# Attention over edges: a fourth chunk of weights turned by DMA in heads 4 and 5, and other places for the next tile's loads

## The reference

```python
q = ((x @ Wq[l].T + bq[l]) * scaling).reshape(n, H, DH)
k = (x @ Wk[l].T).reshape(n, H, DH)
v = (x @ Wv[l].T).reshape(n, H, DH)
scores = jnp.einsum('ehd,ehd->eh', q[tgt], k[srcidx])
m = jax.ops.segment_max(scores, tgt, num_segments=n)
p = jnp.exp(scores - m[tgt])
s = jax.ops.segment_sum(p, tgt, num_segments=n)
w = p / (s[tgt] + 1e-16)
agg = jax.ops.segment_sum(w[:, :, None] * v[srcidx], tgt, num_segments=n)
attn = agg.reshape(n, D) @ Wo[l].T + bo[l]
```

## Time and profile before

| | us |
|---|---|
| median of 3 runs | 3416.27 |
| lowest, highest | 3409.2, 3417.36 |
| span of the profiled execution | 3423.3 |
| PE busy in the span | 3052.8 (89%) |
| DVE, POOL, ACT busy | 2274.0, 2149.5, 1953.9 |

### The profile page before, as it was taken

How to read it: one execution, slowest core, us unless ns; L and a number is a source line. 1 busy time by engine, 2 the same in 40 slices (tenths; PEclk the granted TensorE clock), 3 DMA queues, 4 the chain that set the end, 5 groups by cost and what they waited for, 6 DMA issues and landing times. The chain is left out here.

```text
span 3423.3 us, 72330 instructions
## 1 busy us (share of the span) xinstructions
PE 3052.8 (89%) x24802; PEld 2399.2 (70%) x24802; DVE 2274.0 (66%) x6951; ACT 1953.9 (57%) x3918; POOL 2149.5 (63%) x1979
## 2 busy tenths in 40 slices
PE   2368999978869999999999989989999999999985
PEld 2124665545547888888888877767888888888874
DVE  8594433432337888888887853227888888888856
ACT  0124444433337777777777721227777778777724
POOL 1686778777527777777777710007777777777734
PEclk9999999989989999999999999999999999999987
DMA  9666666545589999999999921239999999989851
GB/s 371 98 129 158 124 118 131 113 93 98 90 201 175 166 170 166 170 163 172 163 168 160 156 75 29 52 70 181 169 165 167 166 172 168 169 165 175 151 119 60
DMA packets 1297462, 496.76 MB, mean 145 GB/s; under 512 B 1237240, under 2 KB 1262865, under 8 KB 1291408
## 3 DMA queue, kind: packets, MB, share of 16 engines
q1 hardware_dynamic: 1156197, 460.22, 67.6%
q0 software_dynamic: 133120, 0.80, 4.1%
q10 hardware_dynamic: 7788, 31.21, 2.7%
HBM read 153.55 MB, written 80.48 MB: 68 GB/s over the span
## 5 line engine op out<-in xcount | busy, mean ns | idle before, releaser
L1476 DVE CUSTOM_DVE_ANT_0 prob<-s_ps,mask 125x500 f32<-125x500 f32 x1600 | 1058.9, 673 | 277.8 <-PE s_ps L1323 201.8
L1253 POOL TENSOR_TENSOR staged<-prob,staged 125x500 f16<-125x500 f32 x960 | 1061.7, 1112 | 166.3 <-ACT staged L1247 103.8
L1413 ACT ACTIVATE prob<-prob,neg_max 125x1000 f32<-125x1000 f32 (+1 forms) x960 | 954.6, 994 | 117.5 <-DVE scrap L1482 114.7
L1323 PE MATMUL s_ps<-keys,queries 128*125 128x500 f16 x3200 | 944.5, 377 | 40.3 <-DMA queries<-q_tiles 27.4
L529 POOL DMA_INDIRECT counts<-count,cell x320 | 654.5, 2045 | 257.9 <-issue 96.4
L1354 PEld LDWEIGHTS o_ps<-values,across 125*125 125x125 f16 x7680 | 590.3, 138 | 196.8 <-issue 51.7
L1354 PE MATMUL o_ps<-values,across 125*125 125x128 f16 x7680 | 606.5, 222 | 33.8 <-DMA across<-staged 33.0
L1247 POOL CAST staged<-prob 125x500 f16<-125x500 f32 x640 | 385.5, 602 | 368.2 <-ACT prob L1413 238.5
L1489 DVE TENSOR_TENSOR p_lo<-t_ps,p_hi 125x500 f16<-125x500 f32 x640 | 432.1, 675 | 91.5 <-ACT p_hi L1423 91.1
L1334 PE MATMUL t_ps<-identity,prob 125*125 125x125 f32 x2560 | 411.8, 283 | 2.7 <-ACT agg L1433 2.5
L1423 ACT CAST p_hi<-t_ps 125x500 f16<-125x500 f32 x640 | 361.0, 564 | 85.1 <-PE t_ps L1334 84.5
(11 more groups left out here) (159 smaller groups left out, 3676.2 us busy)
## 6 DMA issues: line engine op xcount, KB each, us to landing
mask<-bias_rows SPq DMA_DIRECT2D x200, 218.8 KB
counts<-xt ACTq DMA_DIRECT2D x8, 3054.0 KB, 37.3
keys<-counts SPq DMA_DIRECT2D x40, 546.9 KB
bias_rows<-edge_bias SPq DMA_DIRECT2D x20, 1093.8 KB
queries<-q_tiles SPq DMA_DIRECT2D x80, 250.0 KB, 3.9
pair_row<-pair_flat SPq DMA_DIRECT2D x40, 437.5 KB
across<-staged SPq DMA_TRANSPOSE x960, 3.3
q_tiles<-q_both SPq DMA_DIRECT2D x80, 125.0 KB, 3.0
```

Source lines behind the costliest of these rows:

```text
L1253: engine.tensor_tensor(here[0:P, BPC:2 * BPC, 0:P], prob[u % PROBS][:, k * KC:(k + 1) * KC].rearrange("p (s c) -> p s c", s=BPC), here[0:P ...
L1323: mm = pe.matmul(s_ps[n % SB][:, 0:KC], lhsT=queries[b][:, h, part, :], rhs=keys[:, h, c * KC:(c + 1) * KC], start=(part == 0), stop=(part ...
L1413: act.activation(here, here, ACT.Exp, bias=neg_max[u % 4][:, :], accum_out=sums[u // H % 2][:, u % H, piece:piece + 1]).then_inc(exped, 1)
L1476: dve.tensor_tensor_reduce(out=prob[u % PROBS][:, at], in0=s_ps[n % SB][:, 0:KC], in1=bias[b][:, at], scale=1.0, scalar=MASKED, op0=ALU.ad ...
```

## The change

In heads 4 and 5 of every tile (`MORE_AT`) chunk 1 is turned by DMA too, and PE turns only chunk 3. POOL makes both halves of chunk 1 in its stage. It signals on the semaphores of chunk 0 (`STAGED_BY`). Counts that were products are now looked up in lists. The rings keep their sizes: three stages, four `across`. The next tile's loads move: the first half of the queries and mask chunk 0 to head 7 of the tile before (for tile 1, to the start), the second half to head 0, mask chunks 1, 2, 3 to heads 1, 2, 3, and chunk 4 to head 5. Head 4 and head 6 load nothing.

```diff
-BY_DMA = (0, 2, 4)
-BY_PE = tuple(k for k in range(NKC) if k not in BY_DMA)
-HIGH_BY = {0: "POOL", 2: "POOL", 4: "ACT"}
-LOW_BY = {0: "POOL", 2: "POOL", 4: "POOL"}
+MORE_AT = (4, 5)
+HIGH_BY = {0: "POOL", 1: "POOL", 2: "POOL", 4: "ACT"}
+STAGED_BY = {0: 0, 1: 0, 2: 2, 4: 4}
...
+def by_dma(u):
+    return (0, 1, 2, 4) if u % H in MORE_AT else (0, 2, 4)
+
+
+def by_pe(u):
+    return tuple(k for k in range(NKC) if k not in by_dma(u))
...
-                        before, chunk = dma_chunk_at(n - ACROSS)
-                        sp.wait_ge(weighted, NKC * before + chunk + 1)
-                    sp.wait_ge(low_staged[k], U0 + u + 1)
+                        sp.wait_ge(weighted, weighted_by(DMA_CHUNKS, n - ACROSS))
+                    sp.wait_ge(low_staged[STAGED_BY[k]], staged_by(u, k))
...
+                def begin_next(t):
+                    if t < NT:
+                        if t > 1:
+                            sp.wait_ge(maxed, U0 + H * (t - 1))
+                        load_queries(t, 0)
+                        load_mask(t, 0)
+
+                def go_on(t, h):
+                    if t < NT:
+                        if h == 0:
+                            load_queries(t, 1)
+                        elif h <= 3:
+                            load_mask(t, h)
+                        elif h == 5:
+                            load_mask(t, 4)
...
                 for u in range(UNITS):
...
+                    t, h = u // H, u % H
+                    if h == H - 1:
+                        begin_next(t + 2)
+                    else:
+                        go_on(t + 1, h)
...
-                    for k in BY_DMA:
+                    for k in by_dma(u):
                         turn(u, k)
...
-                        for k in BY_DMA:
-                            reached(dve, low_staged[k], U0 + u - PROBS + 1)
+                        if u >= PROBS:
+                            for k in by_dma(u - PROBS):
+                                dve.wait_ge(low_staged[STAGED_BY[k]], staged_by(u - PROBS, k))
```

More of the change, by code:

```diff
@@ L87 @@
 ACROSS = 4
+def by_dma(u):
+    return (0, 1, 2, 4) if u % H in MORE_AT else (0, 2, 4)
+def by_pe(u):
+    return tuple(k for k in range(NKC) if k not in by_dma(u))
+DMA_CHUNKS = [(u, k) for u in range(UNITS) for k in by_dma(u)]
+PE_CHUNKS = [(u, k) for u in range(UNITS) for k in by_pe(u)]
+DMA_AT = {chunk: n for n, chunk in enumerate(DMA_CHUNKS)}
+PE_AT = {chunk: n for n, chunk in enumerate(PE_CHUNKS)}
+STAGED_AT = {}
+for signal in (0, 2, 4):
+    for n, chunk in enumerate(c for c in DMA_CHUNKS if STAGED_BY[c[1]] == signal):
+        STAGED_AT[chunk] = n
+STAGED_COUNT = {signal: sum(STAGED_BY[k] == signal for u, k in DMA_CHUNKS) for signal in (0, 2, 4)}
 EXTRA = {(1, 4): ("T", 0), (2, 2): ("T", 1), (3, 2): ("O", 0), (3, 4): ("O", 1), (4, 2): ("O", 2), (4, 4): ("O", 3)}
@@ L93 @@
     for k in range(NKC):
-        if k in BY_PE:
+        if k in by_pe(u):
             USERS.append(("P", u, k))
@@ L1189, in attention @@
         stages_cleared = sem("stages_cleared")
-        high_staged = {k: sem(f"high_staged{k}") for k in BY_DMA}
-        low_staged = {k: sem(f"low_staged{k}") for k in BY_DMA}
+        high_staged = {k: sem(f"high_staged{k}") for k in STAGED_COUNT}
+        low_staged = {k: sem(f"low_staged{k}") for k in STAGED_COUNT}
         crossed = [sem(f"crossed{r}") for r in range(ACROSS)]
@@ L1207, in pe_chunk, with staged_by, weighted_by @@
         def pe_chunk(u, k):
-            return len(BY_PE) * (U0 + u) + BY_PE.index(k)
+            return len(PE_CHUNKS) * layer + PE_AT[u, k]
         def dma_chunk(u, k):
-            return len(BY_DMA) * (U0 + u) + BY_DMA.index(k)
-        def dma_chunk_at(n):
-            return n // len(BY_DMA), BY_DMA[n % len(BY_DMA)]
+            return len(DMA_CHUNKS) * layer + DMA_AT[u, k]
+        def staged_by(u, k):
+            return STAGED_COUNT[STAGED_BY[k]] * layer + STAGED_AT[u, k] + 1
+        def weighted_by(chunks, n):
+            in_layer, n = divmod(n, len(chunks))
+            u, k = chunks[n]
+            return NKC * (UNITS * in_layer + u) + k + 1
         def user_done(engine, n):
@@ L1222, in user_done @@
             if what == "P":
-                engine.wait_ge(bank_read, len(BY_PE) * (UNITS * in_layer + where) + BY_PE.index(part) + 1)
+                engine.wait_ge(bank_read, len(PE_CHUNKS) * in_layer + PE_AT[where, part] + 1)
             elif what == "T":
@@ L1247, in high_to_stage @@
             copy(staged[n % STAGES][0:P, 0:BPC, 0:P],
-                 prob[u % PROBS][:, k * KC:(k + 1) * KC].rearrange("p (s c) -> p s c", s=BPC)).then_inc(high_staged[k], 1)
+                 prob[u % PROBS][:, k * KC:(k + 1) * KC].rearrange("p (s c) -> p s c", s=BPC)).then_inc(high_staged[STAGED_BY[k]], 1)
         def low_to_stage(engine, u, k):
             here = staged[dma_chunk(u, k) % STAGES]
-            engine.wait_ge(high_staged[k], U0 + u + 1)
+            engine.wait_ge(high_staged[STAGED_BY[k]], staged_by(u, k))
             engine.tensor_tensor(here[0:P, BPC:2 * BPC, 0:P],
                                  prob[u % PROBS][:, k * KC:(k + 1) * KC].rearrange("p (s c) -> p s c", s=BPC),
-                                 here[0:P, 0:BPC, 0:P], ALU.subtract).then_inc(low_staged[k], 1)
+                                 here[0:P, 0:BPC, 0:P], ALU.subtract).then_inc(low_staged[STAGED_BY[k]], 1)
         with nc.Block() as block:
@@ L1259, in _, with load_queries @@
             def _(sp):
[L1260 to L1263, removed]
+                def load_queries(t, half):
+                    sp.dma_start(queries[t % 2][64 * half:64 * half + 64, :, :, :].rearrange("d h s n -> d (h s n)"),
+                                 q_tiles[t * DH:(t + 1) * DH, :]).then_inc(q_loaded[t % 2], 16)
                 def load_mask(t, c):
@@ L1278, in turn @@
                                            ).then_inc(crossed[n % ACROSS], 16)
-                load_queries(0)
+                def begin_next(t):
[12 more added lines that the diff above has]
+                            load_mask(t, 4)
+                for half in range(2):
+                    load_queries(0, half)
                 for c in range(NKC):
                     load_mask(0, c)
+                begin_next(1)
                 for u in range(UNITS):
[L1284 to L1295, removed]
-                    for k in BY_DMA:
+                    t, h = u // H, u % H
[3 more added lines that the diff above has]
+                        go_on(t + 1, h)
+                    if t == 0 and h == NKC + 1:
+                        sp.dma_start(wo_sb[:, :, :].rearrange("p c d -> p (c d)"), g["wo"][layer * 128:(layer + 1) * 128, :]
+                                     ).then_inc(wo_loaded, 16)
+                    for k in by_dma(u):
                         turn(u, k)
@@ L1303, in _ @@
                 for u in range(UNITS):
-                    for k in BY_DMA:
+                    for k in by_dma(u):
                         if HIGH_BY[k] == "POOL":
                             high_to_stage(pool, pool.tensor_copy, u, k)
-                        if LOW_BY[k] == "POOL":
-                            low_to_stage(pool, u, k)
+                        low_to_stage(pool, u, k)
             @block.tensor
@@ L1420, in high_half @@
                     if m >= PB:
-                        unit, at = divmod(m - PB, len(BY_PE))
-                        act.wait_ge(weighted, NKC * unit + BY_PE[at] + 1)
+                        act.wait_ge(weighted, weighted_by(PE_CHUNKS, m - PB))
                     act.copy(p_hi[m % PB][:, :], t_ps[r][0:P, 0:KC]).then_inc(p_high, 1)
@@ L1468, in add_bias @@
                             dve.wait_ge(mask_loaded[b], BOTH * NKC * ((T0 + u // H) // 2 + 1))
-                        for k in BY_DMA:
-                            reached(dve, low_staged[k], U0 + u - PROBS + 1)
+                        if u >= PROBS:
+                            for k in by_dma(u - PROBS):
+                                dve.wait_ge(low_staged[STAGED_BY[k]], staged_by(u - PROBS, k))
+                        elif layer > 0:
+                            for signal in STAGED_COUNT:
+                                dve.wait_ge(low_staged[signal], STAGED_COUNT[signal] * layer)
                         apart(dve, g["waits_met"])
@@ L1522, in statistics @@
                                      xt[:, o, c * CH:(c + 1) * CH]).then_inc(bn_chunks, 1)
[L1524 to L1528, removed]
                 for u in range(2):
@@ L1533, in _ @@
                     maximum(u)
-                for step in range(NKC):
-                    stage_lows(0, step)
                 for u in range(UNITS):
@@ L1543, in _ @@
                             read_low(u - 1)
-                        stage_lows(u, k + NKC)
-                        if u + 1 < UNITS:
-                            stage_lows(u + 1, k)
                         step = extra_before(u, k)
```

## The result

The changed kernel takes 3568.6 us (median of four) where the kernel before, timed beside it, takes 3415.9: a ratio of 1.0452, with a 95% interval of 1.0436 to 1.0468, or 153 us more. Three of its four executions took 3564.6 to 3571.1 us; the fourth took 5299.5 at a granted clock of 0.556, where the others had 0.968, and the ratio leaves it out. Its profiled execution has a span of 3568.9 us. Forecast were 3500 and a range of 3400 to 3575: the sign and the mechanism held, the forecast size was 84 us of the 153.

What follows compares the result with a forecast made beforehand. PE looked like the bound, with the three-stage staging ring a second loop close behind. A tile going from 48.9 to 51.0 us, +2.1 over 40 tiles, adds 84 us: 3500 in the runs, range 3400 to 3575.

Steps and rivals of the forecast that it cites:

- The ring of three stages: Staging buffers filled, subtracted, issued, landed, refilled: a second loop beside PE, needing 45.0 us of a 48.9 us tile.
- The length of a turn: One stage's cycle: copy to end of subtraction 1.79, issue 0.20, landing 3.51, next copy 0.12; sum 5.62 us.
- the 3.9 us that I called spare: Per tile in the kernel before: tile of 48.9 us against 45.0 us for 8 turns on three stages.
- The turns: Staging: 26 chunks instead of 24 on three stages, 8.67 turns of 5.62 us, 48.7 us a tile if never idle.
- six tenths: Share of the spare 3.9 us taken to remain, 2.3 us, giving 51.0 us a tile; ends 48.7 and 52.6.
- The held copy: ACT's copy of chunk 4 in heads 4 and 5 waits for chunk 0's landing: 1 to 3 us, twice a tile.
- It holds: SP with two more issues of 1.44 us: from 40.9 to 43.8 us of a tile, still carried.
- rival D: The DMA engines fill, queues form and landings grow by perhaps 0.3 us, to over 3.7: 3604 us; chance 0.10.
- DMA share higher: Expected sign in the changed kernel: the DMA engines' share above the 0.93 of the stretch before.
- The moved loads: Same 12 issues in other heads: counted as nothing; PE's waits for transposes, at most 23 us in all, could be won.
- PE's 39 us: Chunk 1's PE transposes gone in heads 4 and 5: 80 x 0.49 us, all exposed while PE is the bound.
- Rival A: Landings hide, PE's 39 us come out: 3377 us; needs a turn under 5.52 us; chance 0.18.

## Why the prediction was right, and what it mis-sized

**The bound.** The ring of three stages as a second loop beside PE was right, and it was read from one landing and one copy 0.15 us behind it. It was more than that already: a fourth stage gave the kernel before 35 us, where PE's waits for transposes were to be worth 23 at most.

**The length of a turn.** 5.62 us lies beside the 5.55 of the run with two stages, but that is in part luck: landings were shorter there (3.35 us), and the time still holds 0.19 us of wait. In the kernel before a turn took 6.09 us on average. Of its distance from 5.62, 0.28 us is a stage standing free (0.40 less my 0.12 for the next copy), the rest is the issue (0.28, I had estimated 0.20), the fill (1.86, not 1.79) and the landing (3.55, not 3.51). So only 2.2 of the 3.9 us that I called spare were idle stages.

**The turns.** 26 / 3 turns of 5.62 are 48.7 us, and the tile took 52.5. The term that I mis-sized is the idle time that the ring keeps: I took 2.3 of 3.9 us, six tenths between two ends with no row for it, and 3.8 was left over my turns. That was my upper end (52.6), and is the difference between 84 and 144 us. By the table 1.7 of these 3.8 us are stages standing free in the changed kernel (8.67 x 0.20), and the other 2.1 are turns that take longer than I had summed, which no full ring would have filled. Why the 1.7 remain can only be argued: a delay in the ring may come back to it through the exponentials, which come in PE's rhythm, since PE waits for the ring.

**The held copy.** Right as a row, though larger than the 1 to 3 us that I saw: on average over the inner tiles ACT's wait grew from 0.7 to 3.1 us in head 4 and from 0.3 to 4.3 in head 5, the longest of all heads. Wrong as a cause. It was my reason for the larger share; with the copy moved to POOL the time stays (3579).

**POOL, SP, DMA.** "It holds" was right for the load, as the run with transposes beside four stages shows. It was wrong to count nothing: with three stages two more issues are delays in the ring, 67 us by themselves. In the changed kernel they may overlap with what the two more stage uses cost: its issue part grew by 0.06 us a turn only, some 20 us in all. Landings did not grow (3.55 us on average before and after, and D wanted over 3.7), so rival D is out. The sign "DMA share higher" did not come, since the tile grew with the transposes.

**The moved loads.** I took nothing. Alone they cost 26 us, through the ring: 0.08 us more a turn, 8 turns, 40 tiles. Beside the fourth chunk no such cost is seen. The sum for the whole change was hardly touched.

**PE's 39 us.** The size is about right where the rings are wide: from the kernel before with four stages to the changed one with four stages and five `across`, PE's busy time falls by 0.83 us a tile (47.57 to 46.74), of my 0.98. Its idle time rises by 0.24 (0.27 to 0.51). That the 39 us would be "all exposed as long as PE is the bound" was too much: 17 came out. In the changed kernel itself PE's busy time doesn't fall (3069.6 us after 3052.8), and why it doesn't stays open.

**The rule weighed.** The Trainium skill, page DMA: Bandwidth & Descriptors, section Rules for kernel authors, says to issue a DMA early and wait on its semaphore late, so that its fixed cost overlaps. Here the buffer waits as well, and the runs side with the row: the same chunks take 3569 us with three stages and 3391 with four.

**Rival A** wanted landings under 3.41 us and a ring with room. It had neither: they took 3.55.

## What to carry to other kernels

Before work is moved to a path of copy, transfer and use, count its buffers: turn time over number of buffers is the path's rate, however idle its engines look. The turn is read from starts and landings, not from the releaser that a view names, and over many chunks rather than one: a sum of the parts that I had read put this ring at 92% of a tile (45.0 of 48.9 us), where most of its copies already waited for a landing. In such a ring room comes first and load second: one more buffer was worth 178 us to the changed kernel and 35 to the kernel before, the load that it should carry at most 17.

## What the runs showed that I had not expected

The kernel before was itself paced by the ring to a good part, although PE was busy 98% of the stretch: 58% of its stage copies start right behind a landing, and with a fourth stage PE's idle time falls from 0.8 to 0.3 us a tile.

Two transposes a tile that nobody waits for cost 67 us with three stages and nothing with four, at a DMA share of 1.04. A share of 1 of the 16 engines is thus no bound by itself here: PE was busy 99.5% of the stretch beside it.
